# Local attention tiles: normalise the probabilities first, swap the value product's operands, add the rotation's halves on GpSimd

## The reference

```python
h = shift_token(x)                      # second half of the features from the token before
q, k, v = split(h @ wqkv)               # 8 heads of 64
q = l2norm(q) * qs ; k = l2norm(k) * ksc        # divide by max(norm, 1e-12)
q = q*cos*scale + rotate_half(q)*sin*scale      # the rotation; k with 1/scale
sim = where(masked, -big, 8 * q @ k.T)          # band: j <= i <= j + 64
o = softmax(sim) @ v                            # 8 heads of 64 side by side = 512
x = x + o @ wo
h = layernorm(shift_token(x)) * lg + lb         # variance + 1e-5
x = x + (a * gelu(g)) @ w2 + b2                 # a, g = split(h @ w1 + b1)
```

## Time and profile before

| | us |
|---|---|
| median of 3 runs | 428.27 (425.56 to 429.67) |
| the profiled execution | 427.02 |
| its span, first to last instruction | 425.2 |
| granted TensorE clock, mean | 0.967 of full speed |

### The profile page before, as it was taken

The page is one execution under the profiler, slowest core; times in us unless marked ns, Lnnn a source line. Parts: engine busy times, 40 slices in busy tenths (PEclk is TensorE's granted clock), DMA queues, the critical chain, the costliest instruction groups (busy, mean ns, idle before and its releaser), DMA issues.

```text
span 425.2 us, 10200 instructions
## 1 busy us (share of the span) xinstructions
PE 367.1 (86%) x4097; PEld 269.5 (63%) x4100; DVE 349.1 (82%) x721; ACT 289.6 (68%) x602; POOL 22.8 (5%) x30
## 2 busy tenths in 40 slices
PE   2899999999636779997878999999999999997866
PEld 1498788886511335554446766877767687776855
DVE  5989978986888999978799989888797988884543
ACT  1789998884344457766655766867868787776642
POOL 2000020000011040000000000000000002020110
PEclk9999999999955999999999999999999999998998
DMA  8700010000000000000000000000000000000000
GB/s 328 305 4 4 3 40 5 3 4 3 1 0 0 2 0 2 2 2 0 2 1 2 0 2 0 2 2 0 2 2 1 2 0 2 2 0 2 25 2 25
DMA packets 1774, 8.30 MB, mean 20 GB/s; under 512 B 192, under 2 KB 448, under 8 KB 1472
## 3 DMA queue, kind: packets, MB, share of 16 engines
q1 hardware_dynamic: 1728, 7.65, 4.5%
HBM read 7.12 MB, written 0.52 MB: 18 GB/s over the span
## 4 chain that ended last, share of the span: by engine, by line
PE 44%; DVE 35%; ACT 14%; issue 5%; DMA 1%; DVEq 0%; ACTq 0%
PE ps L252 12%; PE ps L655 5%; ACT blk L1349 3%; DVE blk L1167 3%; DVE blk L1158 3%; DVE lneg L1183 3%; DVE ss L1168 3%; DVE blk L1176 3%; PE ps L567 2%; PE ps L628 2%; PE ps L505 2%; PE ps L609 2%; DVE stats L821 2%; PE ps L619 2%; PE ps L697 2%
## 5 line engine op out<-in xcount | busy, mean ns | idle before, releaser
L567 PE MATMUL ps<-w_f,full 128*128 128x512 f32 x96 | 44.8, 600 | 0.9 <-issue 0.9
L1467 ACT ACTIVATE PT<-ps,lneg 128x128 f32<-128x128 f32 x128 | 34.7, 382 | 10.5 <-DVE lneg L1183 10.5
L628 PEld LDWEIGHTS ps<-blk,PT 128*128 128x128 f32 x256 | 30.3, 192 | 0.6
L628 PE MATMUL ps<-blk,PT 128*128 128x65 f32 x256 | 30.4, 272 | 0.0
L252 PEld LDWEIGHTS ps<-blk,st 128*128 128x128 bf16 x768 | 26.8, 98 | 3.8
L1158 DVE TENSOR_TENSOR blk<-ps,tabs 128x1024 f32<-128x1024 f32 x16 | 19.6, 1223 | 10.6 <-ACT blk L1434 10.6
L252 PE MATMUL ps<-blk,rel 128*128 128x64 bf16 x768 | 27.6, 193 | 0.0
L252 PE MATMUL ps<-blk,st 128*128 128x64 bf16 x768 | 27.6, 193 | 0.0
L1019 DVE TENSOR_REDUCE mneg<-ps 128x4 bf16<-128x512 bf16 x32 | 21.9, 687 | 6.6 <-PE ps L357 6.4
L567 PEld LDWEIGHTS ps<-w_f,full 128*128 128x128 f32 x96 | 16.9, 190 | 16.3 <-issue 16.2
L1520 ACT ACTIVATE PT<-ps 128x512 f32<-128x512 f32 x32 | 17.4, 594 | 12.9 <-PE ps L505 12.9
(11 more groups left out here) (235 smaller groups left out, 908.0 us busy)
## 6 DMA issues: line engine op xcount, KB each, us to landing
w_f<-f_dram SPq DMA_DIRECT2D x2, 1689.0 KB, 13.2
w_x<-l_dram SPq DMA_DIRECT2D x1, 774.0 KB, 5.9
w_f<-ffn_dram SPq DMA_DIRECT2D x1, 561.0 KB, 7.9
X<-x_dram SPq DMA_DIRECT2D x1, 512.0 KB, 3.6
ctxT<-ctxT_dram SPq DMA_DIRECT2D x1, 512.0 KB, 4.4
OT<-maskT_dram SPq DMA_DIRECT2D x1, 512.0 KB, 7.1
rest<-l_dram SPq DMA_DIRECT2D x1, 385.0 KB, 4.4
const<-const_dram SPq DMA_DIRECT2D x1, 324.0 KB, 6.3
```

What stands on the lines that cost most here:

```text
L567: m = mm(ps[:, c, :], hT[:, n, :], w_f[:, l, F_QKV + 512 * c:F_QKV + 512 * (c + 1)], start=True, stop=True)
L628: m = mm(ps[:, 5 + h // 4, 65 * (h % 4):65 * (h % 4 + 1)], P1[:, i % 2, P * h:P * (h + 1)], VL[:, i % 3, s, :], start=(h % 4 == 0), stop=T ...
L1467: e = a(S1[:, i % 2, P * k:P * (k + 1)], ps[:, 3 + c, P * j:P * (j + 1)], ACT.Exp, bias=lneg[:, i % 2, k:k + 1])
```

## The change

Six edits, all about the local tiles but for the norm's epsilon:

1. The Exp instructions also write out the sum of each row (`accum_out`, to `lsum`). `normalise_p` on DVE takes the reciprocals and multiplies the probabilities, in two halves of four heads, before `turn_p`; `divide_output` is gone, and the column of ones with it.
2. `weigh` swaps its operands: V (64 columns) is loaded and the turned probabilities (128 columns) stream; even heads write partitions 0 to 63 and odd heads 64 to 127 of bank 5. The result is already turned, so `turn_o` is gone. `weigh` waits for both halves of P1.
3. ACT copies that result (`take_turned_o(i-1)`) first in iteration i, in front of the Exps; `take_lower_half` moves behind them. `project_o(i-1)` stands where `turn_o` stood.
4. R + T2 moves from DVE to GpSimd (`sum_pairs`), two per quarter in front of the bias work. `unit_norm` waits for it, and `rotate` for the one before.
5. On DVE the order in an iteration is now: `unit_norm`, `quarter_rows`, first half of `normalise_p`, `add_down`, second half, `rotate`, `add_output`, `quarter_moments`.
6. The lower bound of the sums of squares and the variance plus epsilon were `tensor_scalar` instructions; each becomes a `tensor_reduce` over pairs of which one member is the constant (`ss_floor`, `mv[:, :, 2]`).

Cut to its core (buffers, constants and the same wait under a new name are left out):

```diff
-            def turn_o(i):
-                pe.wait_ge(sem("lo_norm"), i + 1)
+            def project_o(i):
+                pe.wait_ge(sem("loT"), i + 1)
                 if i >= 1:
                     pe.wait_ge(sem("z"), i)
                 else:
                     pe.wait_ge(sem("res_added"), 6)
                 for j in range(4):
-                    t = tr(ps[:, 7, P * j:P * (j + 1)], LO[:, i % 2, P * j:P * (j + 1)], ident)
-                t.then_inc(sem("loT_ps"), 1)
-
-            def project_o(i):
-                pe.wait_ge(sem("loT"), i + 1)
-                for j in range(4):
                     m = mm(ps[:, 7, 0:P], LOT[:, j, :], w_f[:, i // NB, F_WO + P * j:F_WO + P * (j + 1)],
                            start=(j == 0), stop=(j == 3))
                 m.then_inc(sem("lwo_ps"), 1)
...
-                    pe.wait_ge(sem("lexp"), 2 * i + c + 1)
+                    pe.wait_ge(sem("p_norm"), 2 * i + c + 1)
...
             def weigh(i):
                 pe.wait_ge(sem("qkv_read"), i + 1)
+                pe.wait_ge(sem("p_turned"), 2 * i + 2)
                 for h in range(LH):
-                    if h % 4 == 0:
-                        pe.wait_ge(sem("p_turned"), 2 * i + h // 4 + 1)
-                    s = 2 * (h % 4) + h // 4
-                    m = mm(ps[:, 5 + h // 4, 65 * (h % 4):65 * (h % 4 + 1)], P1[:, i % 2, P * h:P * (h + 1)],
-                           VL[:, i % 3, s, :], start=(h % 4 == 0), stop=True, skip_group_check=True)
+                    j, c = h // 2, h % 2
+                    m = mm(ps[64 * c:64 * (c + 1), 5, P * j:P * (j + 1)], VL[:, i % 3, h, :],
+                           P1[:, i % 2, P * (4 * c + j):P * (4 * c + j + 1)],
+                           start=(j == 0), stop=True, skip_group_check=True)
                 m.then_inc(sem("lo_ps"), 1)
...
-                    turn_o(i - 1)
+                    project_o(i - 1)
...
-                if i >= 1:
-                    project_o(i - 1)
...
-                v.tensor_scalar(ve[:, lo:hi], mv[:, lo:hi, 1], EPS, None, ALU.add).then_inc(sem("ln_var"), 1)
+                v.tensor_reduce(ve[:, lo:hi], mv[:, lo:hi, 1:3], AX.X, ALU.add).then_inc(sem("ln_var"), 1)
...
+                if i >= 1:
+                    dve.wait_ge(sem("pair_sum"), i)
...
-                settle()
-                dve.wait_ge(sem("rotated"), i + 1)
-                step(v.tensor_tensor(R[:, i % 2, :], R[:, i % 2, :], T2, ALU.add))
-                step(v.tensor_reduce(ss[:, :], SQ.rearrange("p (h j) -> p h j", j=LD), AX.X, ALU.add))
-                settle()
-                v.tensor_scalar(ss[:, :], ss[:, :], 1e-24, None, ALU.max).then_inc(sem("ss"), 1)
+                step(v.tensor_reduce(ss_floor[:, :, 0], SQ.rearrange("p (h j) -> p h j", j=LD), AX.X, ALU.add))
+                settle()
+                v.tensor_reduce(ss[:, :], ss_floor[:, :, :], AX.X, ALU.max).then_inc(sem("ss"), 1)
 
             def unit_norm(i):
                 dve.wait_ge(sem("root"), i + 1)
+                dve.wait_ge(sem("pair_sum"), i + 1)
                 newton(ss[:, :], lr0[:, :], lnt, lr[:, :])
...
-            def divide_output(i):
-                dve.wait_ge(sem("lo_ps"), i + 1)
-                o = ps[:, 5:7, 0:260].rearrange("p b (h d) -> p b h d", h=4)
-                step(v.reciprocal(lrec[:, :].rearrange("p (b h) -> p b h", b=2), o[:, :, :, LD]))
-                settle()
-                if i >= 2:
-                    dve.wait_ge(sem("loT_ps"), i - 1)
-                v.tensor_tensor(LO[:, i % 2, :].rearrange("p (h b d) -> p b h d", b=2, h=4), o[:, :, :, 0:LD],
-                                lrec[:, :].rearrange("p (b h o) -> p b h o", b=2, h=4).to_broadcast([P, 2, 4, LD]),
-                                ALU.mult).then_inc(sem("lo_norm"), 1)
+            def normalise_p(i, c):
+                dve.wait_ge(sem("lexp"), 2 * i + c + 1)
+                r = lrec[:, 4 * c:4 * c + 4]
+                step(v.reciprocal(r, lsum[:, i % 2, 4 * c:4 * c + 4]))
+                settle()
+                p = S1[:, i % 2, 512 * c:512 * (c + 1)].rearrange("p (h k) -> p h k", h=4)
+                v.tensor_tensor(p, p, r.rearrange("p (h o) -> p h o", o=1).to_broadcast([P, 4, P]), ALU.mult)\
+                    .then_inc(sem("p_norm"), 1)
...
-                if i >= 1:
-                    divide_output(i - 1)
                 if 2 <= i + 1 < 2 * NB:
                     unit_norm(i + 1)
+                if i >= 4 and i % 2 == 0:
+                    quarter_rows((i - 4) // 2)
+                normalise_p(i, 0)
                 if i >= 5 and i % 2 == 1:
                     add_down((i - 5) // 2)
-                if i >= 4 and i % 2 == 0:
-                    quarter_rows((i - 4) // 2)
+                normalise_p(i, 1)
                 if i == 1:
                     normalise(6, X, Z, "z_in", 4, NB)
                 if i + 2 < 2 * NB:
...
+                if i >= 1:
+                    add_output(i - 1)
                 if i >= 3 and i % 2 == 1:
                     quarter_moments((i - 3) // 2)
-                if i >= 1:
-                    add_output(i - 1)
...
-                act.wait_ge(sem("loT_ps"), i + 1)
+                act.wait_ge(sem("lo_ps"), i + 1)
                 if i >= 1:
                     act.wait_ge(sem("lwo_ps"), i)
-                a(LOT, ps[:, 7, :].rearrange("p (j t) -> p j t", j=4), ACT.Copy).then_inc(sem("loT"), 1)
+                a(LOT, ps[:, 5, :].rearrange("p (j t) -> p j t", j=4), ACT.Copy).then_inc(sem("loT"), 1)
...
-                              bias=lneg[:, i % 2, k:k + 1])
+                              bias=lneg[:, i % 2, k:k + 1], accum_out=lsum[:, i % 2, k:k + 1])
...
-                if i >= 3 and i % 2 == 1:
-                    take_lower_half((i - 3) // 2)
+                if i >= 1:
+                    take_turned_o(i - 1)
                 exponential(i)
...
                 if i >= 3 and i % 2 == 1:
+                    take_lower_half((i - 3) // 2)
                     take_shifted_half((i - 3) // 2)
...
+            def sum_pairs(i):
+                pool.wait_ge(sem("rotated"), i + 1)
+                g_.tensor_tensor(R[:, i % 2, :], R[:, i % 2, :], T2, ALU.add).then_inc(sem("pair_sum"), 1)
+
+            for i in range(4):
+                sum_pairs(i)
             for q in range(8):
+                for i in range(4 + 2 * q, min(6 + 2 * q, 2 * NB)):
+                    sum_pairs(i)
                 l, j = divmod(q, 4)
```

More of the change, by code:

```diff
@@ L141, in build @@
         stats = sb("stats", [NB, 6])
-        mv = sb("mv", [NB, 2])
+        mv = sb("mv", [NB, 3])
         ve = sb("ve", [NB])
@@ L153, in build @@
         ymax = sb("ymax", [2])
-        ones = sb("ones", [P])
         wq_i = sb("wq_i", [2, 3, P], BF16)
@@ L175, in build @@
         ss = sb("ss", [2 * LH])
+        ss_floor = sb("ss_floor", [2 * LH, 2])
         lss = sb("lss", [2 * LH])
@@ L179, in build @@
         lr = sb("lr", [2 * LH])
+        lsum = sb("lsum", [2, LH])
         lrec = sb("lrec", [LH])
@@ L216, in build @@
         KT = view(blkf, 7168, 2, 4, P)
-        VL = view(blkf, 9216, 3, LH, LD + 1)
-        LO = view(blkf, 10776, 2, 512)
+        VL = view(blkf, 9216, 3, LH, LD)
         LOT = full[:, 0, 0:512].rearrange("p (a b) -> p a b", a=4)
@@ L575, in turn_qk @@
                 elif i >= 2:
-                    pe.wait_ge(sem("lo_norm"), i - 1)
+                    pe.wait_ge(sem("loT"), i - 1)
                 else:
@@ L674, in last_hidden @@
                 pe.wait_ge(sem("yT"), 14)
-                pe.wait_ge(sem("lo_norm"), 2 * NB)
+                pe.wait_ge(sem("loT"), 2 * NB)
                 for t in range(3):
@@ L784, in _ @@
             turn_norm(16, 6)
-            turn_o(2 * NB - 1)
             hidden_wait(16, 6)
@@ L816, in norm @@
                 normalise(k, src, dst, name, lo, hi)
+            step(v.memset(mv[:, :, 2:3], EPS))
+            settle()
             def moments(k, src, lo, hi):
@@ L823, in moments @@
                 for n in range(lo, hi):
-                    step(v.bn_aggr(mv[:, n, :], stats[:, n, :]))
+                    step(v.bn_aggr(mv[:, n, 0:2], stats[:, n, :]))
                 settle()
-                v.tensor_scalar(ve[:, lo:hi], mv[:, lo:hi, 1], EPS, None, ALU.add).then_inc(sem("ln_var"), 1)
+                v.tensor_reduce(ve[:, lo:hi], mv[:, lo:hi, 1:3], AX.X, ALU.add).then_inc(sem("ln_var"), 1)
             def normalise(k, src, dst, name, lo, hi):
@@ L963, in quantise_weight @@
                 quantise(src, inv, tmp, out, "wq")
-            step(v.memset(ones[:, :], 1.0))
             step(v.memset(less_magic[:, :], -MAGIC))
             step(v.memset(wsc[:, :], 1.0))
+            step(v.memset(ss_floor[:, :, :], 1e-24))
             step(v.memset(hmax[:, :], 0.0))
@@ L1256, in _ @@
                     moments(6, X, 4, NB)
+                if i >= 1:
+                    add_output(i - 1)
                 if i >= 3 and i % 2 == 1:
                     quarter_moments((i - 3) // 2)
```

(13 more changed lines are left out.)

## The result

The changed kernel takes 416.15 us (median of 4 runs, 414.26 to 417.55) against 428.24 us before; the ratio is 0.971, 95% interval 0.967 to 0.975. Forecast were 418 us and a range of 409 to 429. The profiled execution of the changed kernel took 417.55 us with a span of 415.8, against a span of 425.2 before.

What follows compares the result with a forecast made beforehand. It took one loop through TensorE, ScalarE and VectorE to bound each 24.56 us pair. Savings of 6.3 (pairs), 1.5, 1.2 and 1.1 total 10.1 us: execution 427.0 to 416.9, plus 1.3 for the median, 418; range 409 to 429.

Steps and rivals of the forecast that it cites:

- a: What a row sum adds to the spacing of two Exps on ScalarE; taken as 0.14 us, possible values 0.075 to 0.33.
- loop V: Loop per pair of tiles starting over VectorE, from maxima through Newton step, normalising and gelus: 22.1 + 8a, forecast 23.2 us.
- loop S: Loop per pair of tiles over ScalarE and TensorE, with both groups of eight Exps: 20.9 + 16a, forecast 23.1 us.
- The row sums: Sums written by ScalarE's Exps, the term without a profile row: 0.14 us each, eight Exps in 3.3 us.
- The dear row sums: Rival: row sums on ScalarE cost up to 0.33 us each, total 441 us, slower; chance 0.09.
- The add on GpSimd: R + T2 leaves VectorE's loop (1.31 us, mostly 1.23) and takes 2.37 us on GpSimd, covered by other VectorE work.
- The rival of a locked-out sum: Rival: GpSimd's sum is locked out and takes 4.8 us, pairs 25.0, total 435 us; chance 0.07.
- The value product: TensorE's eight products with swapped operands overlap on two array halves: 1.1 to 1.3 us instead of 1.73.
- Division against normalising: On VectorE 0.9 us of division goes, 1.6 of reciprocals and products comes; balance with the add -0.5 per tile.
- The small edits: Bounds as pairs on VectorE cost the same 0.17 us; two instructions at the end, no longer held up, give 1.1 back.
- this loop: The old kernel's chain per pair through TensorE, ScalarE's squares and VectorE; savings count there until the next loop is longer.
- TensorE's clock: Rival: the granted clock falls as TensorE is busy for less of each pair; given nothing.

## Why the prediction was right

The time, 416.15, lies 1.9 below the forecast of 418, and 7.2 above the lower end of the range. Part of that closeness is luck. The five pairs gave 2.2 more than forecast, and the stretches ahead and behind together 2.9 less, so the errors nearly cancel. And the forecast set the median 1.3 above the profiled execution, where the median came out 1.4 below it. What held is the mechanism: the loop through VectorE sets the pair. By its steps:

- *The loops.* At the measured a = 0.09 loop V is 22.1 + 0.7 = 22.8 and loop S 22.3. Measured are 22.81, by a chain that visits the stations of loop V, each within 0.12 us of its price. The fifth pair, with GpSimd's two bias instructions, is 0.22 longer where 0.5 was set aside: the first step of the Newton step takes 0.39 instead of 0.17 beside the second of them. Loop V held in the experiments too: 0.6 less without row sums, 2.2 to 2.5 more with the held-up bound.

```profile
350.90 0.72 POOL L1636 TENSOR_TENSOR zv<-zv,X 128x256 f32<-128x256 f32 x1
...
351.27 0.39 DVE L833 TENSOR_TENSOR lnt<-lr 128x16 f32<-128x16 f32 x1
```

- *The row sums* were the mis-sized term: a = 0.14 was forecast and 0.09 measured, near the lower bound of 0.075 from the smallest ScalarE instruction. The bound's reasoning was right, the choice of the middle was not: the read is 0.22 long and overlaps with both neighbours, and 0.22 less the Exps' overlap of 0.127 is the measured 0.09. At 0.09 the five pairs would have been forecast at -8.3; -8.49 was measured. The dear row sums, the rival I gave most to, are out.
- *The add on GpSimd*: 2.36 for 2.37. VectorE never waited for it in the pairs. The rival of a locked-out sum did not happen: in the pairs no VectorE instruction with two SBUF inputs ran beside the sum. Where one ran beside a bias instruction of GpSimd, it was held up (the 1.62 and the 0.39 above).
- *The value product*: 1.09 for 1.1 to 1.3.
- *Division against normalising*: the products of 128 x 512 take 0.69 and not 0.62, but with the reciprocals they fill 1.54 of the chain where 1.6 was forecast. VectorE's balance of -0.5 per tile is what the windows show, 20.05 for 21.05 per pair.
- *The small edits*: L820, the epsilon, is at 0.16 at the end too. What I priced as 1.1 us at the end is worth 15.7 us, as the bound of each tile would have been held up by the sum. I had costed the edit against the trace of before, in which no sum ran on GpSimd, instead of against the new neighbour.
- *What bounds the kernel before.* "A saving counts where it lies in this loop, and until the next loop is longer": the add's move alone shows that the next loop, mostly TensorE's own, was as long. Which of the two set the pair before can't be told; either way the add alone gives nothing. I had summed only loops of the changed order and so didn't see that the 1.31 would be worth nothing per pair without TensorE's relief. The two edits carry each other: the move alone brings 0 per pair, the rest alone costs 1.3 to 2.4, both together bring 1.75.
- *Ahead of tile 4* the gain was overrated, 1.2 for 2.7. With the move alone tiles 0 to 4 took 41.43, with the whole change 42.56, so the rest of it takes 1.1 back there. The forecast had charged the row sums with 0.8 for the four tiles together, where the run without them shows up to 3.4. The granted clock is a term that it lacked: its mean over these tiles was 1.00 before, with the move alone and without row sums, but 0.96 in the changed kernel; in the run with the waits filled, which is the same kernel up to there, it was 0.92 and the tiles took 43.29. From these two executions I estimate 0.7 us for each 0.04.
- *TensorE's clock*: "I give it nothing" holds in the pairs (1.00) and failed ahead of them and behind. The forecast looked at busy shares of a pair, where it should have looked at the single waits: 3.2 and 2.7 us behind the last even tile, and 12 us at 1.2 GHz around and behind the second. The whole stretch came out 0.33 longer instead of 1.1 shorter; filling the waits gave 2.9 back by the medians and 2.8 by the traces.

The median moved by 12.1 and the profiled spans by 9.4; the profiled execution of the changed kernel is the slowest of its four runs. Between the three profiled executions of the changed kernel the difference lies at the start and behind the last even tile, and the pairs repeat to 0.01.

## What to carry to other kernels

When two loops over different engines are equally long, relief of one is worth nothing until the other is relieved too: sum each loop of the order as it stands, and the one that remains when an edit has taken its part. A place where two engines' work ends at the same moment, as at L1196 here, is the sign of it. When work moves to GpSimd, look at every VectorE instruction that will then run beside it, down to the smallest, and give it a form that isn't held up. Waits of TensorE of 2 or 3 us, as near the end of this kernel, can cost twice, once as a wait and once as a slow clock behind it; the filler here helped only where it stood ahead of the instruction that waits.

## What the runs showed of the hardware

- A row sum written out by an Exp of 128 columns appears as an instruction of 0.22 us, but adds only 0.09 us to the distance of two Exps (0.345 against 0.255).
- A VectorE instruction with one SBUF input and a constant on 16 columns took 1.30 us beside GpSimd's two-input add, until that ended, and a reduction over pairs that gives the same result 0.19. This agrees with the Trainium skill ("SBUF — State Buffer", "Who interferes with whom"), by which `tensor_scalar` can contend with GpSimd and `tensor_reduce` never does.
- A VectorE add with two SBUF inputs took 1.62 us instead of 1.23 beside a GpSimd add of 0.73, and a small product of that kind 0.39 instead of 0.17 beside one of 0.72.
- Eight fp32 products of 128 columns with 64 loaded columns took 1.09 us when neighbours used different halves of the array and 1.58 when one half's came ahead of the other's, a factor of 1.45 by the order alone. Four products of 128 columns with 128 loaded take 1.09, so eight would be 2.2, and against that the alternating order is about twice as fast. This agrees with the "up to 2x" of the Trainium skill ("TensorEngine Tiling (Array Packing)", "Theoretical Speedup").
- The granted clock fell at waits of TensorE of 1.83 us inside the loop of one experiment and of 2.7 us at the end of the changed kernel. It did not fall at one of 2.19 in the first pair of the same experiment, nor in the profiled execution of the result at the one of 3.17. With unread products at the start of the two last waits it stayed at 1.00 through them.
